# Expert jobs: the next expert's turned rows are split ahead of its weight tile in tiles 8, 10, 12 and 14

## The chip, the cores and the metric

The kernel runs on one core of one Trainium2 chip. The metric is the device time of one execution in microseconds (us); less is better. A time given for a kernel is the median of several executions, and the trace comes from one further execution taken with the profiler. Times in the trace count from the first instruction of that execution.

## The reference

The reference is a perceiver block on 16 sequences of 64 tokens of width 512 (1024 tokens in all). It has three residual stages, each on a layer norm of `x`:

```python
x = x + xattn(layernorm(x), ctx, ctx, ...)   # 16 heads of 64, 512 keys a sequence, layer norm of its own at the end
x = x + attn(layernorm(x), ...)              # 16 heads of 32, 3D rotary positions
x = x + ffn(layernorm(x), ...)               # 8 experts, the best 2 per token
```

The last one is the stage that this change touches:

```python
logits = xf @ Wr + br                        # xf: 1024 x 512, E = 8 experts
topv, _ = lax.top_k(logits, 2)
masked = jnp.where(logits >= topv[:, 1:2], logits, -jnp.inf)
weights = jax.nn.softmax(masked, axis=-1)
h = jax.nn.gelu(jnp.einsum('td,edh->eth', xf, W1) + b1[:, None, :], approximate=False)   # hidden width 2048
expert_out = jnp.einsum('eth,ehd->etd', h, W2) + b2[:, None, :]
out = jnp.einsum('etd,te->td', expert_out, weights)
```

## The kernel before

Every engine has a program of its own, written out in order (`tensor_program`, `vector_program`, `scalar_program`, `gpsimd_program`, `sync_program`), and the programs meet in semaphores. An engine works strictly through its list: what stands behind a waiting instruction waits too. Matrix products are made of float32 numbers split into a high and a low part in the type fp32r (three products: high by high, high by low, low by high). ScalarE writes the high part of an operand (a rounding copy), VectorE the low part (source minus high part). Each weight tile, each set of gathered rows and each hidden tile is split in this way.

The first 1180 us of the trace are the two attention stages and the routing, which writes for each expert a list of its tokens' rows to memory (`expert_rows`). Then come eight **jobs**, one for each expert `q`, numbered 0 to 7. A job is made for a number of rows (its width) that PE picks from `WIDTHS` by the count of this expert's tokens. In the profiled execution the matmuls of jobs 1, 3 and 5 are 224 wide, those of job 6 128, those of jobs 0, 2, 4 and 7 288, 512, 448 and 336.

A job goes over 16 **tiles** `i` of 128 hidden columns. In tile `i`:

- PE does `up(q, i)`: 12 matmuls (L448) of the expert's turned rows `xgT` with weight tile `Wh[i]` into a bank of PSUM, then `down(q, i-3)` (L809), 3 matmuls for each 128 rows of the width, of an older hidden tile, and in tiles 8, 10, 12 and 14 `turn_rows(q+1, c)`, c = 0 to 3: four transposes (L453) of 128 gathered rows `xg[c]` of the **next** expert, all into bank 7.
- ScalarE does the gelu of the bank (L1607), then in tiles 4 to 15 `split_next(q+1, i-4)`, the high part of the next expert's weight tile (L1314); in tiles 0 to 3 these are the last four of its own expert. In tiles 8, 10, 12 and 14 `rows_high(q+1, c)` (L1581) copies the turned rows out of bank 7.
- VectorE does the high and low part of the gelu's result (`hs`, L1275 and L1277), then `split_low` of the same weight tile (L888), and in tiles 8, 10, 12 and 14 `rows_low(q+1, c)` (L1254), the low part of the turned rows.

Which waits hold this together:

- `split_next` waits for the weight tile in its raw buffer (`raw`, four buffers in turn, loaded by SyncE's queue at L310) and for `down` to have left the slot `Wh[i]`. A raw buffer is loaded anew once `split_low` has read it.
- `rows_high` waits for the transposes of its chunk; `rows_low` waits for `rows_high`. Since all chunks are turned in bank 7, `turn_rows` of chunk c waits for `rows_low` of chunk c-1 (`xgT_lo`), and for its rows from memory.
- `up` of tile `i` waits for the gelu of tile `i-3`, `down(q, i-3)` for VectorE's L1277 of that hidden tile.

Of the kernel before, what the change touches and what calls it, by code (L numbers as in the profile page):

```python
# [19 lines left out]
def perceiver_block(nc, a, out):  # L20
# [17 lines left out]
    with ExitStack() as stack:  # L38
# [193 lines left out]
        def w_load(q, i):  # L232
            return L_E + q * NI + i
# [55 lines left out]
        def turned_at(i):  # L289
            return {8: 0, 10: 1, 12: 2, 14: 3}.get(i)  # L290
# [4 lines left out]
        def sent(t):  # L295

            return 16 * E * (t // 3 + 1) - (16 if t >= NT - 2 else 0)

        def turn_bank(q, c):

            return bank[3 + c] if q == 0 else bank[7]
# [580 lines left out]
        def vector_program(v):  # L882
            def split_lo(n, lo, hi):

                r = raw_of[n]
                src = raw[r][:] if len(lo.shape) == 2 else raw[r][:].rearrange("p (a b) -> p a b", a=lo.shape[1])
                v.wait_ge(split_hi, n + 1)
                v.tensor_tensor(lo, src, hi, ALU.subtract).then_inc(split_done[r], 1)  # L888
# [285 lines left out]
            def split_low(q, i):  # L1174
                split_lo(w_load(q, i), Wh[i][1][:], Wh[i][0][:])
# [74 lines left out]
            def rows_low(q, c):  # L1250
                src = turn_bank(q, c).rearrange("p (k z) -> p k z", k=KD)
                hi, lo = (x[:, :, c * P:(c + 1) * P] for x in xgT[q % 2])
                v.wait_ge(xgT_hi, CH * q + c + 1)
                v.tensor_tensor(lo, src, hi, ALU.subtract).then_inc(xgT_lo, 1)  # L1254

            def weighted(q):

                for c in range(CH):
                    if q == E - 1:  # L1260
                        v.wait_ge(y_ready, q + c + 1)
                    elif c == 0:
                        v.wait_ge(y_ready, q + 1 if q < E else q + CH)
                    else:
                        v.wait_ge(y_psum, NI * (q + 1))
                    v.wait_ge(ys_bias, CH * q + c + 1)
                    v.scalar_tensor_tensor(ys[c][:], bank[3 + c], weight(q, c), ys[c][:], ALU.mult, ALU.add).then_inc(y_done, 1)  # L1267

            def job(q, more):

                for i in range(NI):
                    n = NI * q + i
                    hi, lo = (x[:] for x in hs[n % HS])
                    v.wait_ge(gelu_done, n + 1)
                    v.tensor_copy(hi, gl[n % HS][:]).then_inc(h_hi, 1)  # L1275
                    v.wait_ge(h_hi, n + 1)
                    v.tensor_tensor(lo, gl[n % HS][:], hi, ALU.subtract).then_inc(h_lo, 1)  # L1277
                    if q == 0 and i < 3:
                        split_low(0, 10 + 2 * i)
                        split_low(0, 11 + 2 * i)  # L1280
                    if i > LAG and more:
                        split_low(q + 1, i - LAG - 1)
                    if i <= LAG and q % E:
                        split_low(q, NI + i - LAG - 1)
                    if more and turned_at(i) is not None:
                        rows_low(q + 1, turned_at(i))
                weighted(q)

            split_low(0, 3)
# [19 lines left out]
        def scalar_program(s):  # L1309
            def split_high(n, hi):  # L1310
                r = raw_of[n]
                src = raw[r][:] if len(hi.shape) == 2 else raw[r][:].rearrange("p (a b) -> p a b", a=hi.shape[1])
                s.wait_ge(raw_loaded[r], 16 * (raw_turn[n] + 1))
                s.activation(hi, src, ACT.Copy).then_inc(split_hi, 1)  # L1314
# [140 lines left out]
            def slot_left(i):  # L1455

                if i < 6:
                    s.wait_ge(qkv_psum, 3 * (NT - 1) + i // 2 + 1)
                elif i < 8:
                    s.wait_ge(nxT_psum, NT)  # L1460
                elif i == 8:
                    s.wait_ge(x1_bias, NT)
                    s.wait_ge(v2_done, NT)
                elif i == 9:
                    s.wait_ge(rope_done, 2 * NT)
                    s.wait_ge(s2_psum, 2 * NT)
                    s.wait_ge(o2_psum, NT)
                elif i == 10:
                    s.wait_ge(s2_psum, 2 * NT)
                    s.wait_ge(o2_psum, NT)  # L1470
                elif i < 13:
                    s.wait_ge(d_psum, NT)
                elif i == 13:
                    s.wait_ge(rows_sent[(NT - 1) % 3], sent(NT - 1))
                    s.wait_ge(rope_done, 2 * NT)
                    s.wait_ge(lg_psum, NT)
                elif i == 14:
                    s.wait_ge(rope_done, 2 * NT)
                    s.wait_ge(qkT_psum, 2 * NT)
                    s.wait_ge(lg_psum, NT)  # L1480
                else:
                    s.wait_ge(o2_psum, NT)
                    s.wait_ge(out_seeded, SEEDS)
                    s.wait_ge(e_norm, NT)

            def split_first(i):
                slot_left(i)
                split_high(w_load(0, i), Wh[i][0][:])
# [85 lines left out]
            def rows_high(q, c):  # L1574
                src = turn_bank(q, c).rearrange("p (k z) -> p k z", k=KD)
                if c == 0 and q >= 2:
                    s.wait_ge(h_psum, NI * (q - 1))
                elif c == 0:
                    s.wait_ge(qkv_psum, 3 * NT)
                s.wait_ge(xgT_psum, CH * q + c + 1)  # L1580
                s.activation(xgT[q % 2][0][:, :, c * P:(c + 1) * P], src, ACT.Copy).then_inc(xgT_hi, 1)  # L1581
# [16 lines left out]
            def job(q, more):  # L1598
                for i in range(NI):
                    n = NI * q + i  # L1600
                    col = (q % E) * NI + i
                    s.wait_ge(h_psum, n + 1)
                    if n == 0:
                        s.wait_ge(rows_sent[(NT - 2) % 3], sent(NT - 2))
                    if n >= HS:
                        s.wait_ge(y_psum, n - HS + 1)
                    s.activation(gl[n % HS][:], bank[n % 3], ACT.Gelu, bias=b1c[:, col:col + 1]).then_inc(gelu_done, 1)  # L1607
                    if q == 0 and i < 3:
                        split_first(10 + 2 * i)
                        split_first(11 + 2 * i)  # L1610
                    if i > LAG and more:
                        split_next(q + 1, i - LAG - 1)
                    if i <= LAG and q % E:
                        split_next(q, NI + i - LAG - 1)
                    if more and turned_at(i) is not None:
                        rows_high(q + 1, turned_at(i))
                weighted_bias(q, more)

            split_first(4)
# [286 lines left out]
```

## Time and profile before

| what | value |
|---|---|
| median of 3 executions | 1703.01 us |
| the three executions | 1698.38, 1703.01, 1706.31 us |
| the profiled execution's own time | 1704.67 us |
| its span, first to last instruction | 1702.7 us |
| mean granted TensorE clock | 0.974 |
| PE busy | 1618.6 us, 95% |
| VectorE (DVE) busy | 1184.5 us, 70% |
| ScalarE (ACT) busy | 970.7 us, 57% |
| GpSimd (POOL) busy | 355.7 us, 21% |

The span is the time between first and last instruction on the core; 2.0 us of the execution lie around it. In the rows further down, a row of a timeline has its start, its duration, the engine, the line, the operation, what it writes and reads, how many instructions it merges, and in brackets how long the engine was idle ahead of it and what it had waited for. The granted clock is the share of TensorE's full clock: 1.00 is 2.4 GHz, 0.50 is 1.2 GHz.

### The profile page before, as it was taken

How to read it: one execution, taken by the hardware profiler on the slowest of the kernel's cores; microseconds unless marked ns; L12 is line 12 of the kernel's file. 1: busy time of each engine (PE TensorE's matmuls, PEld its weight loads, DVE VectorE, ACT ScalarE, POOL GpSimd, SP SyncE). 2: the span in 40 equal slices, each digit the busy share in tenths (PEclk: the TensorE clock that was granted, in tenths of full speed). 3: DMA queues.
4: the chain of work that ended last, by engine and by line, in shares of the span. 5: the costliest groups of instructions: out<-in, count | busy, mean ns of one | idle time of the engine just before them, and what ended most of it. 6: DMA issues, size and time to landing. Idle time of an engine off the chain costs nothing. (4 is left out here: it accounts for less than half of the span.)

```text
span 1702.7 us, 27762 instructions
## 1 busy us (share of the span) xinstructions
PE 1618.6 (95%) x10730; PEld 1364.5 (80%) x10730; DVE 1184.5 (70%) x2032; ACT 970.7 (57%) x1792; POOL 355.7 (21%) x264
## 2 busy tenths in 40 slices
PE   7999999999999999999999979994899999999987
PEld 6888888888888888888888867773788888888876
DVE  4477777777778778777777776775778448548842
ACT  5566666766666666666666554442556346346631
POOL 4111111211212122112121134656211011011101
PEclk9999999999999999999999999995999999999799
DMA  6572111211211112113112152224757337537711
GB/s 228 191 132 55 50 38 51 94 63 38 82 63 46 61 63 81 38 51 105 51 38 81 38 171 64 65 78 149 245 156 215 131 89 243 159 86 246 217 39 21
DMA packets 60892, 175.20 MB, mean 103 GB/s; under 512 B 10996, under 2 KB 11380, under 8 KB 60192
## 3 DMA queue, kind: packets, MB, share of 16 engines
q1 hardware_dynamic: 45712, 143.97, 25.2%
q0 software_dynamic: 15024, 29.09, 7.9%
q8 instruction: 105, 1.72, 0.4%
q14 instruction: 51, 0.42, 0.1%
HBM read 155.63 MB, written 53.54 MB: 123 GB/s over the span
## 5 line engine op out<-in xcount | busy, mean ns | idle before, releaser
L448 PE MATMUL psum<-ctx,Wk 128*128 128x512 f32 x1536 | 384.6, 399 | 0.0
L448 PE MATMUL psum<-Wv,ctx 128*128 128x512 f32 x1536 | 368.9, 389 | 0.0
L448 PEld LDWEIGHTS psum<-Wv,ctx 128*128 128x128 f32 x1536 | 288.3, 188 | 59.9
L448 PEld LDWEIGHTS psum<-ctx,Wk 128*128 128x128 f32 x1536 | 279.1, 188 | 55.4
L1018 DVE SCALAR_TENSOR_TENSOR kT<-psum,bkc,kT 64x512 fp32r<-64x512 f32 x256 | 191.9, 749 | 151.5 <-ACT kT L1413 147.0
L448 PE MATMUL psum<-xgT,Wh 128*128 128x224 f32 (+5 forms) x1536 | 252.1, 318 | 14.1 <-issue 8.4
L448 PEld LDWEIGHTS psum<-xgT,Wh 128*128 128x128 f32 x1536 | 229.8, 198 | 33.6 <-issue 15.3
L809 PE MATMUL psum<-Wh,hs 128*128 128x512 f32 x981 | 246.6, 397 | 0.0
L1426 ACT ACTIVATE Pr<-Pr,smn 128x512 f32<-128x512 f32 x128 | 92.7, 724 | 241.4 <-DVE smn L1027 241.4
L1413 ACT ACTIVATE kT<-psum,bkc 64x512 fp32r<-64x512 f32 x256 | 174.3, 681 | 61.3 <-PE psum L448 57.9
L809 PEld LDWEIGHTS psum<-Wh,hs 128*128 128x128 f32 x981 | 181.5, 191 | 34.1 <-DVE hs L1277 0.3
L1607 ACT ACTIVATE gl<-psum,b1c 128x512 f32<-128x512 f32 x128 | 87.8, 687 | 202.0 <-PE psum L448 201.7
L1025 DVE TENSOR_TENSOR Pr<-psum,Pr 64x512 f32<-64x512 f32 x256 | 176.3, 689 | 8.0
L888 DVE TENSOR_TENSOR Wh<-raw,Wh 128x1024 fp32r<-128x1024 f32 x128 | 155.7, 1219 | 15.6 <-ACT Wh L1314 15.6
L1314 ACT ACTIVATE Wh<-raw 128x1024 fp32r<-128x1024 f32 x128 | 134.5, 1055 | 42.0 <-DMA raw<-in_W 41.8
L1643 POOL TENSOR_TENSOR Wo<-raw,Wo 128x1024 fp32r<-128x1024 f32 x32 | 76.8, 2400 | 386.3 <-ACT Wo L1314 386.3
L1421 ACT ACTIVATE Pr<-psum 64x512 f32<-64x512 f32 x256 | 151.9, 593 | 6.2
L1275 DVE CAST hs<-gl 128x512 fp32r<-128x512 f32 x128 | 55.3, 432 | 127.4 <-ACT gl L1607 126.9
L1643 POOL TENSOR_TENSOR ctx<-raw,ctx 128x1024 fp32r<-128x1024 f32 x32 | 76.8, 2400 | 288.5 <-ACT ctx L1314 288.5
L1797 POOL DMA_INDIRECT out_x<-xg,meta x22 | 36.3, 1649 | 382.3 <-DVE xg L1267 379.6
L955 DVE TENSOR_TENSOR V<-psum,bvb 128x512 f32<-128x512 f32 x128 | 88.5, 691 | 5.5 <-PE psum L448 1.5
L1277 DVE TENSOR_TENSOR hs<-gl,hs 128x512 fp32r<-128x512 f32 x128 | 88.7, 693 | 4.4
(155 smaller groups left out, 1975.9 us busy)
## 6 DMA issues: line engine op xcount, KB each, us to landing
raw<-in_W SPq DMA_DIRECT2D x128, 512.0 KB, 4.3
expert_rows<-in_spare_rows SPq DMA_DIRECT2D x16, 1042.0 KB, 5.7
raw<-in_ctxT SPq DMA_DIRECT2D x32, 512.0 KB, 3.7
raw<-in_Wo SPq DMA_DIRECT2D x32, 512.0 KB, 3.6
xg<-expert_rows POOLq DMA_DIRECT2D x32, 256.0 KB, 6.2
out_x<-x SPq DMA_DIRECT2D x12, 256.0 KB, 2.4
xs<-in_x SPq DMA_DIRECT2D x4, 512.0 KB, 6.0
raw<-in_Wq SPq DMA_DIRECT2D x4, 512.0 KB, 6.6
```

The costliest lines, as they stand in the source:

```text
L448: mm = pe.matmul(dst, l, r, start=n == 0, stop=n == len(pairs) - 1)
L809: mm = pe.matmul(bank[3 + c], hr[x][:, c * P:(c + 1) * P], Wh[i][y][:, 512:1024], start=i == 0 and m == 0, stop=i == NI - 1 and m == 2)
L888: v.tensor_tensor(lo, src, hi, ALU.subtract).then_inc(split_done[r], 1)
L955: v.tensor_tensor(V[u % 2][:, kt, :], bank[2 + n % 2], bvb[:, cs], ALU.add).then_inc(v_done, 1)
L1018: v.scalar_tensor_tensor(k[other, :], bank[n % 2][own, :], bkc[own, j:j + 1], k[own, :], ALU.add, ALU.subtract).then_inc(k_lo, 1)
L1025: v.tensor_tensor(Pr[m % 2][rows, :], bank[4 + h][rows, :], Pr[m % 2][rows, :], ALU.add).then_inc(s_max, 1)
L1277: v.tensor_tensor(lo, gl[n % HS][:], hi, ALU.subtract).then_inc(h_lo, 1)
L1314: s.activation(hi, src, ACT.Copy).then_inc(split_hi, 1)
L1413: s.activation(kT[n % 2][h][own, :], bank[n % 2][own, :], ACT.Identity, bias=bkc[own, j:j + 1]).then_inc(k_hi, 1)
L1421: s.activation(Pr[m % 2][rows, :], bank[4 + h][other, :], ACT.Copy).then_inc(s_exp, 1)
L1426: s.activation(Pr[m % 2][:], Pr[m % 2][:], ACT.Exp, bias=smn[:, r:r + 1], accum_out=ssum[:, r:r + 1]).then_inc(s_exp, 1)
L1643: g.tensor_tensor(lo, src, hi, ALU.subtract).then_inc(split_done[r], 1)
```

## The change

In tiles 8, 10, 12 and 14 of a job, which have both a weight tile to split and a chunk of turned rows, the two change places on ScalarE and on VectorE: the turned rows come first, the weight tile second. Nothing is added or removed, and PE's, GpSimd's and SyncE's programs are the same.

```diff
@@ VectorE, job(q, more), loop over i
+                    if more and turned_at(i) is not None:
+                        rows_low(q + 1, turned_at(i))
                     if i > LAG and more:
                         split_low(q + 1, i - LAG - 1)
                     if i <= LAG and q % E:
                         split_low(q, NI + i - LAG - 1)
-                    if more and turned_at(i) is not None:
-                        rows_low(q + 1, turned_at(i))
@@ ScalarE, job(q, more), loop over i
+                    if more and turned_at(i) is not None:
+                        rows_high(q + 1, turned_at(i))
                     if i > LAG and more:
                         split_next(q + 1, i - LAG - 1)
                     if i <= LAG and q % E:
                         split_next(q, NI + i - LAG - 1)
-                    if more and turned_at(i) is not None:
-                        rows_high(q + 1, turned_at(i))
```

ScalarE, tiles 7 to 10 of job 6, as the program of before has them. `gl` is a gelu's result, `Wh40` the high part of the next expert's weight tile 4, `raw` its raw buffer, `xgT10` the high part of the next expert's turned rows.

```order
L1607 ACTIVATE gl3_203<-psum,b1c_50 128x512
L1314 ACTIVATE Wh30_174<-raw1_84 128x1024
L1607 ACTIVATE gl0_200<-psum,b1c_50 128x512
L1314 ACTIVATE Wh40_176<-raw2_85 128x1024
L1581 ACTIVATE xgT10_162<-psum 128x4x128
L1607 ACTIVATE gl1_201<-psum,b1c_50 128x512
L1314 ACTIVATE Wh50_178<-raw3_86 128x1024
L1607 ACTIVATE gl2_202<-psum,b1c_50 128x512
L1314 ACTIVATE Wh60_180<-raw0_83 128x1024
L1581 ACTIVATE xgT10_162<-psum 128x4x128
```

The same place on ScalarE in the changed program:

```order
L1607 ACTIVATE gl3_203<-psum,b1c_50 128x512
L1314 ACTIVATE Wh30_174<-raw1_84 128x1024
L1607 ACTIVATE gl0_200<-psum,b1c_50 128x512
L1581 ACTIVATE xgT10_162<-psum 128x4x128
L1314 ACTIVATE Wh40_176<-raw2_85 128x1024
L1607 ACTIVATE gl1_201<-psum,b1c_50 128x512
L1314 ACTIVATE Wh50_178<-raw3_86 128x1024
L1607 ACTIVATE gl2_202<-psum,b1c_50 128x512
L1581 ACTIVATE xgT10_162<-psum 128x4x128
L1314 ACTIVATE Wh60_180<-raw0_83 128x1024
```

The copy of the turned rows (L1581) moved ahead of weight tiles 4 and 6 and directly behind the gelu; weight tiles 3 and 5 stay.

VectorE, tiles 8 and 9 of job 6, before. `hs` are the two parts of the hidden tile, `Wh41` and `xgT11` low parts.

```order
L888 TENSOR_TENSOR Wh31_175<-raw1_84,Wh30_174 128x1024
L1275 CAST hs00_204<-gl0_200 128x512
L1277 TENSOR_TENSOR hs01_205<-gl0_200,hs00_204 128x512
L888 TENSOR_TENSOR Wh41_177<-raw2_85,Wh40_176 128x1024
L1254 TENSOR_TENSOR xgT11_163<-psum,xgT10_162 128x4x128
L1275 CAST hs10_206<-gl1_201 128x512
```

The same place on VectorE in the changed program:

```order
L888 TENSOR_TENSOR Wh31_175<-raw1_84,Wh30_174 128x1024
L1275 CAST hs00_204<-gl0_200 128x512
L1277 TENSOR_TENSOR hs01_205<-gl0_200,hs00_204 128x512
L1254 TENSOR_TENSOR xgT11_163<-psum,xgT10_162 128x4x128
L888 TENSOR_TENSOR Wh41_177<-raw2_85,Wh40_176 128x1024
L1275 CAST hs10_206<-gl1_201 128x512
```

The low part of the turned rows (L1254), for which PE's next four transposes wait, moved ahead of the low part of the weight tile (L888), for which the raw buffer's next load waits.

## Rows read from the trace of the kernel before

**Rows 1.** The page, part 1: engine, busy us, share of the span, instructions.
```profile
PE 1618.6 (95%) x10730; PEld 1364.5 (80%) x10730; DVE 1184.5 (70%) x2032; ACT 970.7 (57%) x1792; POOL 355.7 (21%) x264
```

**Rows 2.** Waits, 1226 to 1572 us (jobs 0 to 5): total us, times, longest.
```profile
ACT xgT L1581 <- PE psum L453: 18.1, 20, 1.6
ACT Wh L1314 <- DMA raw<-in_W: 16.4, 11, 3.2
...
PE psum L453 <- DMA xg<-expert_rows: 0.3, 1, 0.3
```

**Rows 3.** Waits, 1566 to 1625 us (job 6), same columns.
```profile
PE psum L453 <- DVE xgT L1254: 4.0, 1, 4.0
```

**Rows 4.** Chain of waits, 1560 to 1640 us: start, us, what.
```profile
1587.35 8.33 DMA raw<-in_W
```

**Rows 5.** Timeline of ScalarE, job 6, tiles 7 to 8.
```profile
1593.11 1.06 ACT L1314 ACTIVATE Wh<-raw 128x1024 fp32r<-128x1024 f32 x1 [4.33 <-DMA raw<-in_W]
1594.07 0.67 ACT L1607 ACTIVATE gl<-psum,b1c 128x512 f32<-128x512 f32 x1
1595.76 1.06 ACT L1314 ACTIVATE Wh<-raw 128x1024 fp32r<-128x1024 f32 x1 [1.01 <-DMA raw<-in_W]
1596.72 0.58 ACT L1581 ACTIVATE xgT<-psum 128x512 fp32r<-128x512 f32 x1
```

**Rows 6.** Timeline of VectorE, job 6, tile 8 and the start of tile 9.
```profile
1595.34 0.42 DVE L1275 CAST hs<-gl 128x512 fp32r<-128x512 f32 x1
1595.80 0.69 DVE L1277 TENSOR_TENSOR hs<-gl,hs 128x512 fp32r<-128x512 f32 x1
1596.85 1.23 DVE L888 TENSOR_TENSOR Wh<-raw,Wh 128x1024 fp32r<-128x1024 f32 x1 [0.36 <-ACT Wh L1314]
1597.99 0.68 DVE L1254 TENSOR_TENSOR xgT<-psum,xgT 128x512 fp32r<-128x512 f32 x1
1598.59 0.42 DVE L1275 CAST hs<-gl 128x512 fp32r<-128x512 f32 x1
```

**Rows 7.** Timeline of PE, job 6: turn of chunk 0, the last down, turn of chunk 1.
```profile
1590.17 0.60 PE L453 MATMUL psum<-ident,xg 128*128 128x128 f32 x4
...
1593.93 0.92 PE L809 MATMUL psum<-Wh,hs 128*128 128x512 f32 x3
1598.82 1.08 PE L453 MATMUL psum<-ident,xg 128*128 128x128 f32 x4 [3.97 <-DVE xgT L1254]
```

**Rows 8.** Stretches of job 6; behind the busy times: granted clock, DMA share, GB/s.
```profile
1594.00:1597.00 3.00, 0.85 (x4) 0.36 (x3) 2.41 (x4) 1.99 (x4) 0.00 (x0) 1.00 0.87 341
1597.00:1598.80 1.80, 0.00 (x0) 0.01 (x1) 1.80 (x3) 1.80 (x4) 0.00 (x0) 0.54 0.71 282
1598.80:1617.00 18.20, 18.18 (x74) 16.83 (x75) 13.55 (x20) 9.17 (x13) 0.00 (x0) 0.50 0.55 175
1617.00:1621.00 4.00, 4.00 (x23) 3.38 (x23) 2.94 (x5) 2.92 (x5) 0.00 (x0) 0.92 0.37 134
```

**Rows 9.** Timeline of PE, job 0: two other idle gaps.
```profile
1200.27 2.43 PE L448 MATMUL psum<-xgT,Wh 128*128 128x288 f32 x12 [3.13 <-ACT gl L1607]
...
1215.97 1.82 PE L448 MATMUL psum<-xgT,Wh 128*128 128x288 f32 x12 [1.80 <-ACT gl L1607]
```

**Rows 10.** Stretches of job 0 around and behind these gaps, columns as in Rows 8.
```profile
1200.00:1205.00 5.00, 4.73 (x19) 4.25 (x20) 1.79 (x3) 1.43 (x3) 0.26 (x1) 0.66 0.91 323
1210.00:1216.00 6.00, 4.20 (x25) 3.41 (x23) 3.29 (x5) 2.87 (x4) 0.00 (x0) 1.00 1.00 320
1216.00:1221.00 5.00, 5.00 (x31) 4.56 (x32) 4.90 (x9) 4.51 (x6) 0.00 (x0) 1.00 0.85 317
```

**Rows 11.** Timeline of VectorE, job 6, tiles 1 and 2: start of each tile.
```profile
1578.32 0.42 DVE L1275 CAST hs<-gl 128x512 fp32r<-128x512 f32 x1
...
1580.52 0.42 DVE L1275 CAST hs<-gl 128x512 fp32r<-128x512 f32 x1
```

**Rows 12.** Timeline of PE: first product of job 7.
```profile
1627.58 9.38 PE L448 MATMUL psum<-xgT,Wh 128*128 128x336 f32 x48 [6.00 <-issue]
```

**Rows 13.** Timeline of ScalarE, job 1, tile 10 and the gelu of tile 11.
```profile
1287.11 1.06 ACT L1314 ACTIVATE Wh<-raw 128x1024 fp32r<-128x1024 f32 x1
1288.13 0.60 ACT L1581 ACTIVATE xgT<-psum 128x512 fp32r<-128x512 f32 x1
1289.46 0.69 ACT L1607 ACTIVATE gl<-psum,b1c 128x512 f32<-128x512 f32 x1 [0.73 <-PE psum L448]
```

## The prediction

> **What bounds the kernel now.** I read the share of each engine first: PE is busy 95% of the span and no other engine is above 70% [rows 1]. So a change of order on ScalarE and VectorE can only pay where PE waits for them, and can only cost where it makes PE wait. Next I read the waits of the stretch that the change touches, the jobs. In jobs 0 to 5, from tile 8 of job 0 on, the list holds many waits of ScalarE and VectorE for PE, and on PE's own side next to nothing: 0.3 us for gathered rows [rows 2]. In job 6 there is one that matters: PE waits 4.0 us, once, for L1254, the low part of the turned rows [rows 3]. Job 7 turns no rows for a next expert, so the edit is not in it.
>
> The timelines of the three engines tell how that wait comes about. Job 6 is the narrowest, so it asks for weight tiles fastest, and for a while the loads do not keep up: in the chain of waits a load stands for 8.33 us [rows 4]. ScalarE stands 4.33 us ahead of weight tile 3, then does gelu 8, then stands another 1.01 us ahead of weight tile 4; only behind that comes the copy of the turned rows at 1596.72 [rows 5]. Yet chunk 0 had been turned since 1590.17 + 0.60 = 1590.77 [rows 7]. VectorE repeats the order: hidden tile 8, weight tile 4, then the rows at 1597.99 to 1598.67 [rows 6]. PE ended its last down at 1594.85, could go no further than the transposes of chunk 1, and started them at 1598.82, 0.15 after VectorE's end [rows 7]. The last thing to come is thus one weight tile on ScalarE, one weight tile on VectorE, and behind them the two instructions that PE needs. This is the pair that the change turns round.
>
> The stall has a second price. Until 1597 the granted clock is 1.00 (2.4 GHz); in 1597.0 to 1598.8 it is 0.54, so it fell to 1.2 GHz at about 1597.1, some 2.3 us after PE fell idle, and it is 0.50 for the whole 18.2 us behind, in which PE is busy for 18.18 [rows 8]. In the last 4 us of the job it is 0.92. The working below rests on these stretches.
>
> **The change in job 6, step by step.** What stands ahead of tile 8 is the same, so gelu 8 still starts at 1594.07 and hidden tile 8 at 1595.34.
> - ScalarE: the copy of the rows waits for nothing, since chunk 0 is turned. It starts when gelu 8 lets it, about 1594.65, and ends at about 1595.25. Weight tile 4 starts when its load lands, 1595.76, as before: the copy lies wholly in the 1.01 us of idle time [rows 5]. Its cost is nothing here. Without that cover it would push gelu 9 by its own 0.6 us, and PE is not waiting for that gelu.
> - VectorE: L1277 starts at 1595.80, and its successor starts about 0.60 behind it, as 1597.99 to 1598.59 shows for one of the same kind [rows 6]. L1254 therefore runs from 1596.40 to 1597.08 instead of 1597.99 to 1598.67. It fills the 0.36 us that VectorE stood idle there, and L888 comes at 1597.00 instead of 1596.85. The raw buffer is free 0.15 us later, and the next hidden tile starts at 1597.00 + 1.14 = 1598.14 instead of 1598.59.
> - PE: the transposes of chunk 1 start at 1597.08 + 0.15 = 1597.23, which is 1.59 us earlier. The stall goes from 3.97 to 2.38 us. It does not vanish, since what is late next is hidden tile 8 on VectorE (1595.34 to 1596.49), which stands ahead of the rows and itself comes from the 4.33 us wait for weight tile 3, in a tile that the change leaves as it is.
>
> **What the clock does with 1.59 us.** In this profile the clock fell at 1597.1 and PE would come back at 1597.23, so by this execution it falls all the same. The two nearest gaps bound the question: after one of 3.13 us the stretch has 0.66, so there too the clock fell; after one of 1.80 us it stayed at 1.00 [rows 9, 10]. At 2.38 us either can be. I take the fall as the likelier, because 2.38 us still reaches past the point, 2.3 us into the idle time, at which it fell here. With the fall, all that follows until the clock is back is PE at half speed, so 1.59 us less of waiting is 1.59 us less of time if the clock comes back at the same place in the work. If it comes back at the same time, 1.59 us of work at half clock has been taken from a rest that is done at full clock, where it is worth 0.8. I take the middle, **1.2 us**, and keep 0.8 and 1.6 as bounds.
>
> The Trainium skill (TensorE: Matmul & The Clock Gate, Part 1: The HAM clock gate) has it that the low clock is the state of rest, and that sustained matmul activity lifts it. By that rule PE, busy from 1598.8 on, would soon be at full clock again, and a fall would cost no more than a few us; the row of 18.2 us at 0.50 with PE busy throughout says otherwise for this narrow job, and the measurement decides. By the page, the rival without a fall would be worth little more than the 1.6 us of waiting.
>
> **The change in the other jobs.** Take tile 10 of job 1. Before, weight tile 6 ran at 1287.11 to 1288.17 while PE was still turning, the copy followed at 1288.13 to 1288.73, and gelu 11 came at 1289.46 after 0.73 us of idle time [rows 13]. Now ScalarE stands until 1288.13, then does the copy, then the weight tile to about 1289.7, and gelu 11 starts some 0.15 late. PE needs that gelu for `up` of tile 14, three tiles on, so this costs nothing. On VectorE the hidden tile that follows starts up to 0.6 us later, and `down` asks for it three tiles later too. The weight tiles of the next expert are wanted a job later, and a raw buffer freed up to 1.2 us later is wanted again only four tiles on. In the 20 places of this kind where ScalarE waited for the turn, 18.1 us in all and at most 1.6 [rows 2], the weight tile used to be cover for a wait and now isn't; since ScalarE is busy 57% and VectorE 70% [rows 1], I put all of it at **0**, with at most 0.3 us a job either way if a job's end catches one.
>
> **The sum.** The profiled execution took 1704.67 us (span 1702.7 and 2.0 around it). 1704.67 - 1.2 = 1703.5. It lies 1.66 us above the median of 1703.01, so the forecast for a median is 1703.01 - 1.2 = **1701.8 us**.
>
> **The rivals.**
> 1. *The clock does not fall.* Then job 6 goes on at full clock and its pace is VectorE's, not PE's. One tile on VectorE is 1580.52 - 1578.32 = 2.20 us [rows 11], a tile with turned rows 0.60 more. From the cast of tile 9 at 1598.14 to that of tile 15 are six tiles, three of them with rows: 13.2 + 1.8 = 15.0, so 1613.1. Its low part ends 1.15 later at 1614.3, and the last down takes PE to about 1615.2. Before, PE ended the job at 1627.58 - 6.00 = 1621.58 [rows 12]. That is 6.4 us less, 1703.01 - 6.4 = 1696.6 us. For it: 2.38 us is nearer to the gap of 1.80 that left the clock alone than to 3.97. Against it: the point of the fall above.
> 2. *No change.* The stall of 4 us hangs on when single loads land (1593.1 and 1595.8). In an execution where weight tile 4 has landed by the time of gelu 8, the order costs only two weight splits less cover; where a row chunk lands later still, PE waits for that in both kernels. Then nothing moves: 1703.0.
> 3. *Slower: the clock falls and comes back too late.* Before, it came back just in time for the last 4.0 us of job 6. Those 4.0 us less the 0.8 that has been done earlier are 3.2 at full clock and 6.4 at half: job 6 would end at 1617.6 + 6.4 = 1624.0, which is 2.4 us later than before, and the time is 1705.4. It decides at one point: whether the mix of narrow products, downs and transposes, shifted by 1.6 us, brings the clock back before the job ends. For it: the clock stayed low for 18 us of busy PE, so its return is a near thing. Against it: the shift brings more work ahead of the same point.
>
> **How the numbers follow.** The forecast of 1701.8 has a chance of 0.50, rival 1 (1696.6) 0.25, rival 2 (1703.0) 0.13, rival 3 (1705.4) 0.12. The three executions of before spread from 1698.4 to 1706.3, so a median of a few moves by some 2 us by itself. The range takes in rival 1 and rival 3 with a little of that on each side: 1695.5 to 1706.0. A measurement of this kernel can tell about 0.5%, 8.5 us, from no change. A gain over 8.5 us needs rival 1 and a lucky 2 us more: 0.07. A loss over 8.5 us needs rival 3 and several us more: 0.03. The rest, 0.90, is within 0.5%.
>
> **What would show it.** In the profile of the changed kernel, the copy L1581 of job 6, tile 8, should start directly behind its gelu, inside the idle time ahead of the weight tile. PE's wait for L1254 should be about 2.4 us instead of 4.0. Then the granted clock decides: 0.50 over most of the rest of job 6 is the forecast; 1.00, with hidden tiles 2.2 to 2.8 us apart and the job done some 6 us sooner, is rival 1; a job 6 that ends at 0.50 is rival 3. In jobs 0 to 5 PE should show no new idle time. Wrong would be a wait of PE for a gelu or a hidden tile behind tiles 8, 10, 12 or 14 in these jobs, or loads that land so differently that job 6 stalls at another place.

## The result and the profile after

The changed kernel took 1711.61 us (median of 20 executions, 1703.56 to 1722.00) where the kernel before took 1702.99 beside it. The ratio is 1.0050 with a 95% interval of 1.0035 to 1.0065: it is slower, by 0.5%. The forecast was 1701.8 in a range of 1695.5 to 1706.0, so both the size and the side were wrong. One of the 20 executions of the kernel before took 2305.67 us and one of the 12 of e7 below 2036.34 us, far outside the rest, and the ratios leave such executions out.

The profiled execution of the changed kernel took 1720.48 us, span 1718.6. It lies in the upper part of its own 20, so its 15.8 us above the profiled execution of before show where the time goes, not how much of it goes in the median.

The page's first part tells that PE, the engine that bounds the kernel, had 9 us more to do although it has the same instructions [rows 1], which means that more of them ran at the low clock:

```profile
PE 1627.6 (95%) x10730; PEld 1373.1 (80%) x10730; DVE 1187.7 (69%) x2032; ACT 968.8 (56%) x1792; POOL 355.7 (21%) x264
```

The waits that the prediction dealt with are not where the rest is. The list of waits of the changed kernel, 1226 to 1660 us, has no wait of PE for L1254, but this (what waited for what, total us, times, longest):

```profile
PE psum L448 <- issue: 15.8, 5, 6.3
```

"Issue" is idle time in which the engine waited for nothing that the profile shows. The timeline of PE shows where these are: ahead of the first product of jobs 1, 2, 4, 6 and 7. First the kernel before (job 7 is in [rows 12]):

```profile
1261.17 5.59 PE L448 MATMUL psum<-xgT,Wh 128*128 128x224 f32 x48 [0.48 <-issue]
...
1307.47 11.17 PE L448 MATMUL psum<-xgT,Wh 128*128 128x512 f32 x48 [0.85 <-issue]
...
1442.84 9.96 PE L448 MATMUL psum<-xgT,Wh 128*128 128x448 f32 x48 [0.77 <-issue]
...
1573.83 5.54 PE L448 MATMUL psum<-xgT,Wh 128*128 128x128 f32 x48 [0.27 <-issue]
```

and then the changed one:

```profile
1261.23 5.59 PE L448 MATMUL psum<-xgT,Wh 128*128 128x224 f32 x48 [1.70 <-issue]
...
1309.47 13.97 PE L448 MATMUL psum<-xgT,Wh 128*128 128x512 f32 x48 [2.79 <-issue]
...
1449.59 9.96 PE L448 MATMUL psum<-xgT,Wh 128*128 128x448 f32 x48 [2.38 <-issue]
...
1583.50 8.97 PE L448 MATMUL psum<-xgT,Wh 128*128 128x128 f32 x48 [2.60 <-issue]
...
1643.65 8.93 PE L448 MATMUL psum<-xgT,Wh 128*128 128x336 f32 x48 [6.29 <-issue]
```

The first four of these gaps have grown from 2.37 to 9.47 us. In two of the rows the duration has grown too: 48 products of 512 columns take 13.97 us instead of 11.17, 48 of 128 take 8.97 instead of 5.54. The clock fell in or behind the gap (in job 6 it was still 1.00 when the gap ended, and 0.50 from 1585 on). In stretches of the changed kernel (PE busy first, granted clock third from the end) job 6 looks so:

```profile
1580.90:1583.50 2.60, 0.00 (x1) 0.03 (x1) 2.11 (x4) 0.00 (x0) 1.65 (x1) 1.00 0.42 158
...
1585.00:1622.00 37.00, 37.00 (x152) 34.48 (x151) 24.34 (x33) 17.61 (x22) 3.95 (x7) 0.50 0.60 188
1623.00:1633.00 10.00, 10.00 (x78) 9.39 (x77) 9.49 (x14) 8.36 (x12) 0.00 (x0) 1.00 0.48 156
```

```profile
L863 PEldq COMPARE_BRANCH  x1: 3291/3291/3291, 1304.0 to 1304.0; - x1
...
L858 PEldq COMPARE_BRANCH  x1: 3591/3591/3591, 1570.1 to 1570.1; - x1
```

```profile
L863 PEldq COMPARE_BRANCH  x1: 4571/4571/4571, 1304.7 to 1304.7; - x1
...
L858 PEldq COMPARE_BRANCH  x1: 5271/5271/5271, 1578.1 to 1578.1; - x1
```

So in the kernel before these two branches take 3.3 and 3.6 us (the others at the ends of jobs 0 to 5 3.35 to 4.39). In the DMA records one packet of 16 KB of PE's instructions lies within each of them. PE's matmuls of the last tiles, which are queued ahead of the branch, hide most of it. The Trainium skill (Advanced Engine Details and Errata, Control Flow Timing) gives a compare-and-branch about 108 ns; the trace has 65 ns for most of those that are not taken and thirty to fifty times the page's figure for the one that goes to the next job's block. The measurement decides.

Two things have changed at the end of job 1, and both come out of tile 14. The timeline of VectorE at the end of job 1, before and then changed:

```profile
1299.84 1.22 DVE L888 TENSOR_TENSOR Wh<-raw,Wh 128x1024 fp32r<-128x1024 f32 x1
1300.97 0.68 DVE L1254 TENSOR_TENSOR xgT<-psum,xgT 128x512 fp32r<-128x512 f32 x1
1301.93 0.43 DVE L1275 CAST hs<-gl 128x512 fp32r<-128x512 f32 x1 [0.28 <-ACT gl L1607]
1302.39 0.69 DVE L1277 TENSOR_TENSOR hs<-gl,hs 128x512 fp32r<-128x512 f32 x1
```

```profile
1300.57 0.69 DVE L1254 TENSOR_TENSOR xgT<-psum,xgT 128x512 fp32r<-128x512 f32 x1 [0.44 <-ACT xgT L1581]
1301.52 1.23 DVE L888 TENSOR_TENSOR Wh<-raw,Wh 128x1024 fp32r<-128x1024 f32 x1 [0.26 <-ACT Wh L1314]
1302.66 0.42 DVE L1275 CAST hs<-gl 128x512 fp32r<-128x512 f32 x1
1303.11 0.69 DVE L1277 TENSOR_TENSOR hs<-gl,hs 128x512 fp32r<-128x512 f32 x1
```

and ScalarE there, changed:

```profile
1299.94 0.60 ACT L1581 ACTIVATE xgT<-psum 128x512 fp32r<-128x512 f32 x1 [1.15 <-PE psum L453]
1300.43 1.05 ACT L1314 ACTIVATE Wh<-raw 128x1024 fp32r<-128x1024 f32 x1
1301.38 0.68 ACT L1607 ACTIVATE gl<-psum,b1c 128x512 f32<-128x512 f32 x1
```

ScalarE now stands 1.15 us for the turn before it may touch weight tile 10, so both engines finish that tile about 1.7 us later. VectorE starts hidden tile 15 at 1302.66 instead of 1301.93 and is done with it 0.72 us later. PE's program passes its last wait, the one for that tile, only then, and reaches the branch 1.95 us ahead of the end of its matmuls instead of 2.61; the branch starts 0.94 us behind VectorE's end in both kernels. That is the first part. The second: the raw buffer is free later, and the load of weight tile 14 is issued at 1302.77 instead of 1301.08. Timelines of SyncE's queue, 1300 to 1306 us, before and changed:

```profile
1301.08 3.50 SPq L310 DMA_DIRECT2D raw<-in_W  x2
```

```profile
1302.77 2.53 SPq L310 DMA_DIRECT2D raw<-in_W  x2
```

In the DMA records the packet of instructions started 0.92 us into the branch and took 0.88 us before; in the changed kernel it started at 1.12 and took 1.94. At the end of job 5 it started 1.24 us into the branch and took 0.93 before, 2.10 and 1.75 in the changed kernel. So a fetch with a load close ahead of it starts later, or takes longer, or both. What follows the packet is 1.2 to 1.5 us in every such branch of every kernel here.

The gap is what the branch takes less how long ahead it is reached, plus 0.16 us. So the 7.1 us by which the four gaps have grown can be split. The branches of jobs 1, 3 and 5 are reached 0.66, 0.66 and 0.65 us later, 2.0 us in all; those of jobs 0, 1, 3 and 5 take 1.22, 1.28, 0.96 and 1.68 us longer, 5.1 us in all. The branch of job 0 is reached 4.08 us ahead in every kernel of this document, so the late hidden tile plays no part there. The branches at the ends of the wide jobs 2 and 4 took 3.4 to 3.8 us, were reached 3.4 to 3.9 us ahead, and left no gap in either kernel.

### The profile page after: what moved, and what is told of

It reads as the page before. It is cut to its first block and busy times, and to the rows that moved or that the text cites. A ratio compares the mean times of both kernels' runs of the same rounds, so it can differ in the third digit from the quotient of the medians.

```text
span 1718.6 us, 27762 instructions
## 1 busy us (share of the span) xinstructions
PE 1627.6 (95%) x10730; PEld 1373.1 (80%) x10730; DVE 1187.7 (69%) x2032; ACT 968.8 (56%) x1792; POOL 355.7 (21%) x264
## 5 line engine op out<-in xcount | busy, mean ns | idle before, releaser
L448 PE MATMUL psum<-xgT,Wh 128*128 128x224 f32 (+5 forms) x1536 | 261.2, 326 | 22.0 <-issue 15.8
L448 PEld LDWEIGHTS psum<-xgT,Wh 128*128 128x128 f32 x1536 | 238.9, 205 | 42.3 <-issue 22.9
L888 DVE TENSOR_TENSOR Wh<-raw,Wh 128x1024 fp32r<-128x1024 f32 x128 | 155.8, 1220 | 18.7 <-ACT Wh L1314 18.7
L1277 DVE TENSOR_TENSOR hs<-gl,hs 128x512 fp32r<-128x512 f32 x128 | 88.6, 692 | 4.4
```

Of the source, the lines that this page charges most:

```text
L448: mm = pe.matmul(dst, l, r, start=n == 0, stop=n == len(pairs) - 1)
```

## The experiments

The theory has these two parts and a third: (1) hidden tile 15 is late, so the branch is reached late; (2) later loads lie on the fetch, so the branch takes longer; (3) the longer gap lets the clock fall, and in the narrow job 6 it then stays low for long. The rivals of this theory: the loss is spread over all four tiles (raw buffers freed later everywhere), or it is the clock's alone and tied to no place.

For all kernels, from their profiles: PE's idle gap in us at the ends of jobs 0, 1, 3 and 5, how long before the end of PE's matmuls the branch of job 1 began and how long it took, the length of job 6 from its first gelu to that of job 7, and the ratio of the times to the kernel before on the same chip. Gaps, branches and job 6 are those of one profiled execution for each kernel; only the ratio rests on many.

| kernel | gaps, ends of jobs 0, 1, 3, 5 | branch of job 1: ahead, took | job 6 | ratio (95%) |
|---|---|---|---|---|
| before | 0.48, 0.85, 0.77, 0.27 | 2.61, 3.29 | 55.9 | 1 |
| changed | 1.70, 2.79, 2.38, 2.60 | 1.95, 4.57 | 62.0 | 1.0050 (1.0035 to 1.0065) |
| e12, changed again | 1.30, 3.03, 2.00, 1.56 | 1.95, 4.81 | 53.4 | 1.0046 (1.0024 to 1.0068) |
| e1, swap in 8, 10, 12 | 0.43, 1.04, 1.16, 0.74 | 2.61, 3.49 | 48.5 | 0.9999 (0.9982 to 1.0015) |
| e2, swap in 14 | 0.78, 2.92, 1.88, 1.56 | 1.94, 4.65 | 51.1 | 1.0065 (1.0041 to 1.0089) |
| e7, swap on VectorE only | 0.80, 1.90, 2.07, 1.25 | 2.20, 3.94 | 49.8 | 1.0038 (1.0014 to 1.0063) |
| e3, changed, loads held at 1, 3 | 1.19, 1.57, 1.42, 2.67 | 1.85, 3.26 | 62.0 | 1.0050 (1.0028 to 1.0073) |
| e6, changed, loads held at 1, 3, 5 | 0.88, 1.89, 1.58, 0.70 | 1.95, 3.67 | 49.3 | 1.0011 (0.9991 to 1.0031) |
| e4, before, loads held at 1, 3 | 0.50, 1.09, 0.76, 0.33 | 2.52, 3.44 | 49.0 | 1.0000 (0.9982 to 1.0018) |
| e5, e4 and hidden tile 15 late | 0.60, 1.69, 1.83, 0.34 | 1.92, 3.44 | 49.6 | 1.0012 (0.9995 to 1.0029) |
| e8, swap, tile 10 behind 15 | 0.62, 1.21, 1.08, 0.30 | 2.61, 3.65 | 49.7 | 0.9976 (0.9959 to 0.9992) |
| e11, tile 10 behind 15 alone | 0.58, 0.91, 1.31, 0.20 | 2.52, 3.26 | 50.4 | 0.9994 (0.9974 to 1.0014) |
| e9, e1 and no drain | 0.44, 1.55, 1.35, 0.96 | 2.52, 3.90 | 48.6 | 1.0005 (0.9983 to 1.0026) |
| e10, e8 and no drain | 0.74, 1.17, 0.86, 0.06 | 2.61, 3.61 | 47.7 | 0.9966 (0.9951 to 0.9982) |

### Which tile: e1 and e2

Each keeps one part of the swap; the diff is against the kernel before, on both engines, and `(8, 10, 12)` is `(14,)` in the second:

```diff
+                    if more and turned_at(i) is not None and i in (8, 10, 12):
+                        rows_low(q + 1, turned_at(i))
                     if i > LAG and more:
                         split_low(q + 1, i - LAG - 1)
...
-                    if more and turned_at(i) is not None:
+                    if more and turned_at(i) is not None and i not in (8, 10, 12):
                         rows_low(q + 1, turned_at(i))
```

> The swap stays in tiles 8, 10 and 12 and is undone in tile 14. Theory A (the job's end): the loss comes from tile 14 alone, where the later hidden tile 15 lets PE reach its branch to the next job later and the later loads lie on the fetch of that job's instructions. Then PE's gaps at the ends of jobs 0, 1, 3 and 5 are again 0.5, 0.85, 0.8 and 0.3 us (they are 1.7, 2.8, 2.4 and 2.6 in the changed kernel), the branches take 3.3 to 4.4 us, and the time is that of the kernel before or 1 to 3 us less. Rival B (all four tiles count, through raw buffers freed later): three quarters of the loss of 8.6 us stay, about 1709 us.

> The swap stands in tile 14 only. Theory A: all of the loss, 1709 to 1714 us, with gaps of 1.7 to 2.8 us at the ends of jobs 0, 1, 3 and 5. Rival B: a quarter of it, about 1705 us, with gaps that are not much longer than before. Rival C (the loss is the clock's, by chance of where it falls, and not tied to one place): no pattern of gaps.

The swap of three tiles costs nothing that can be measured (0.9999) and that of tile 14 alone costs all of it (1.0065). The gaps follow: 1.04 us at the end of job 1 in e1, 2.92 in e2. (At the end of job 5 e1 has 0.74 where 0.3 was expected; its branch there took 4.04 us.) The rival of four equal tiles is out, and so is the one of the clock alone, since e2's gaps stand at the same places as the changed kernel's. The gain that the first half of theory A allowed for e1, 1 to 3 us, is not to be seen.

### The loads on the fetch: e3, e4 and e6

In e3 (the changed kernel) and e4 (the kernel before) SyncE holds two loads back until PE has done the first product of the next job; e6 is e3 with the end of job 5 as well, `q in (2, 4, 6)`:

```diff
                 for i in range(NI):
+                    if q in (2, 4) and i == 14:
+                        sp.wait_ge(h_psum, NI * q + 1)
                     fetch(w_load(q, i), w12[q, i])
```

> The changed kernel, but the loads of the next expert's weight tiles 14 and 15 at the ends of jobs 1 and 3 wait until PE has done the first product of the next job; jobs 0 and 5 are left as they are. Theory A has two parts: the branch is reached 0.65 us later, and it takes 1.0 to 1.7 us longer because loads share the DMA engines with the fetch of instructions. If the second part holds, the branches at the ends of jobs 1 and 3 take 3.3 us (4.6 and 4.3 in the changed kernel) and the gaps there are about 1.5 us, while the branch at the end of job 5 stays at 4.5 to 5.3 us. If loads don't matter, all stay as long as in the changed kernel.

> The kernel before with the same hold at the ends of jobs 1 and 3. Theory A: branches of 3.3 us as before or a little less, gaps of 0.6 to 0.9 us, time within 0.2% of the kernel before. If the hold itself costs something (a weight tile that comes too late for ScalarE in tile 2 of jobs 2 and 4) it shows here as a wait of ScalarE for a load.

The branch at the end of job 1, e3, then the one at the end of job 5, which was left as it was:

```profile
L865 PEldq COMPARE_BRANCH  x1: 3258/3258/3258, 1306.1 to 1306.1; - x1
...
L860 PEldq COMPARE_BRANCH  x1: 5335/5335/5335, 1574.6 to 1574.6; - x1
```

Where the loads are held the branch takes what it takes in the kernel before, 3.26 us, and 3.33 at the end of job 3 (4.57 and 4.31 in the changed kernel); where they are not, 5.34. One execution holds both cases. The gap at the end of job 1 is 1.57 us, and what is left of it against 0.85 is the first part, the late branch (1.85 us ahead instead of 2.61). The time did not improve, 1.0050: the gap of 2.67 us at the end of job 5 was still there, and job 6 took 62.0 us as in the changed kernel. e4 shows that holding by itself costs nothing that can be measured.

> The changed kernel with the loads held at the end of job 5 as well. Theory: the branch there takes 3.6 us instead of 5.3, the gap is about 1.5 us instead of 2.6, the clock does not fall ahead of job 6, and job 6 takes 48 to 51 us instead of 62. The median comes to 1704 to 1709 us: most of the loss goes with the clock, and what stays is 0.6 us at each of jobs 0, 1, 3 and 5 and the collision at job 0. If the clock falls all the same, job 6 stays at 62 us in the profile and the median at 1711 or more.

The branch of job 5 and PE's first product of job 6 in e6:

```profile
L860 PEldq COMPARE_BRANCH  x1: 3347/3347/3347, 1576.5 to 1576.5; - x1
```

```profile
1580.02 5.55 PE L450 MATMUL psum<-xgT,Wh 128*128 128x128 f32 x48 [0.70 <-issue]
```

and the first part of job 6, stretches of e6:

```profile
1582.00:1594.00 12.00, 12.00 (x94) 11.40 (x94) 10.96 (x15) 8.65 (x12) 4.34 (x6) 1.00 0.94 290
1594.00:1610.00 16.00, 13.73 (x102) 11.97 (x101) 15.35 (x23) 12.30 (x18) 0.94 (x2) 1.00 0.84 295
```

The branch is at 3.35 us, the gap at 0.70 (less than the 1.5 expected, since this branch is reached 2.82 us ahead, those of jobs 1 and 3 1.95 and 2.09), the clock stays at 1.00 and job 6 takes 49.3 us. The ratio went from 1.0050 to 1.0011, which is no longer told from 1; the two intervals barely overlap. Of the two kernels only two loads at the end of job 5 differ in when they may start, so the pair shows part (2), and part (3) in the two profiles. Loads are not all of it: with the loads held, the branches of e5 and e6 at the ends of jobs 1 and 3 still took 3.44 to 3.79 us.

How much of the loss goes through the clock can be read from the single executions, each of which has its mean granted clock on record. In the changed kernel 9 of 20 executions have 0.970 or less, and in e12, the same kernel, 2 of 12; these took 1714.7 to 1722.0 us. The four of the 20 with 0.977 or more took 1703.6 to 1706.3 us, within the spread of the kernel before. Of the 103 executions of the kernel before beside the experiments, 2 have 0.970 or less; of e3's 10 six, of e6's 12 one. So most of what the median lost comes with a lower clock. At which gap it fell in each execution is not on record, except in the profiled ones.

### The late hidden tile: e5 and e7

e5 adds to e4 one VectorE instruction that nobody needs:

```diff
                     v.wait_ge(gelu_done, n + 1)
+                    if i == 15 and q in (1, 3):
+                        v.bn_stats(bst[:, q // 2, :], gl[n % HS][:])
                     v.tensor_copy(hi, gl[n % HS][:]).then_inc(h_hi, 1)
```

> The kernel before with the loads held at the ends of jobs 1 and 3 (so that no load lies on the fetch) and with one needless VectorE instruction of some 0.6 us (statistics of gelu 15, whose result nobody reads) ahead of the cast of hidden tile 15 in jobs 1 and 3. Theory: PE's program reaches its branch only when the low part of hidden tile 15 is there, and PE's queue has nothing behind it, so the gap at the end of the job grows by the delay, one to one: from 1.09 and 0.76 us with the loads held to about 1.7 and 1.4 us, with branches still of 3.3 to 3.5 us; job 5 stays at 0.3. If there is slack between hidden tile 15 and the branch, the gaps stay at 1.1 and 0.8 us.

The gap at the end of job 1 is 1.69 us against 1.09 in e4, with the same branch of 3.44 us, which is reached 0.60 us closer to the end of the matmuls (1.92 for 2.52). So there is no slack between hidden tile 15 and the next job: a delay there is paid one to one. In job 3 the branch was reached 0.60 us closer too (2.13 for 2.73) and took 3.79 for 3.33 on top, for a gap of 1.83 against 0.76; job 5, without the instruction, has 0.34.

e7 has the swap on VectorE and ScalarE's order of before:

> The swap on VectorE alone, ScalarE in the order of the kernel before. Theory: hidden tile 15 is late in the changed kernel because weight tile 10 comes late on ScalarE (it stands there for the turn first) and VectorE's low part of it is queued ahead of hidden tile 15. With ScalarE's old order the cast of hidden tile 15 at the end of job 1 comes some 0.3 us later than before instead of 0.6 to 0.7, PE reaches the branch about 2.3 us ahead of its last matmul, and the loss is about half: median 0 to 0.3% above the kernel before. If VectorE's order alone makes it, the 1.95 us and the full loss stay.

The branch is reached 2.20 us ahead, between the 2.61 of before and the 1.95 of the change, so 0.41 of the 0.66 us is VectorE's order and 0.25 ScalarE's, which stands for the turn with the weight tile behind it; at the end of job 3 it is 0.31 and 0.35. About half each. The ratio of 1.0038 is above the 1.003 I allowed; the branches of jobs 1 and 3 took 3.94 and 4.34 us, so the loads lie on the fetch here too.

### A better order: e8, e11, e9 and e10

e8 keeps all four swaps and takes weight tile 10 out of the way of hidden tile 15, on both engines:

```diff
-                    if i > LAG and more:
+                    if i == 15 and more:
+                        split_low(q + 1, 10)
+                    if i > LAG and i != 14 and more:
                         split_low(q + 1, i - LAG - 1)
```

> The change with one difference: in tile 14 ScalarE and VectorE split the turned rows only, and weight tile 10 follows in tile 15, behind hidden tile 15. So hidden tile 15 is as early as in the kernel before, and the loads of weight tiles 14 and 15 are later than in any kernel so far. Theory: PE reaches its branch 2.6 us ahead of its last matmul at the end of job 1, as in the kernel before, not 1.95 as in the changed one; what is left of the loss is the collision of loads and fetch, branches of 4 to 5 us and gaps of 1.5 to 2.2 us. Median 1703 to 1711 us. If only the late hidden tile counts, gaps are 0.3 to 0.9 us and the median is 1703 to 1706.

> The kernel before, no swap, with weight tile 10 split in tile 15 behind hidden tile 15 on both engines. It tells whether the gain of the version with both (0.24%) is the swap's or this edit's. Theory: before the change, hidden tile 15 waited for its gelu and not for VectorE, so this edit alone gains nothing: 1.000, and PE's stall for the turned rows of job 6 stays at 2 to 4 us. If it gains as much as the two together, the swap has no part in the gain.

e8 is faster than the kernel before, 0.9976 (0.9959 to 0.9992). The branch is reached 2.61 us ahead as before, and the collision that I expected to remain is small: a branch of 3.65 us, and gaps of 1.21, 1.08 and 0.30. That was a miss on my side. The branch at the end of job 1 and the loads behind it, e8 (branches by line, then SyncE's queue, 1307.7 to 1312 us):

```profile
L863 PEldq COMPARE_BRANCH  x1: 3651/3651/3651, 1307.6 to 1307.6; - x1
```

```profile
1307.83 1.46 SPq L310 DMA_DIRECT2D raw<-in_W  x2
```

What counts is where the load before the branch lies. In e8 the two loads are issued 0.23 and 1.36 us behind the start of the branch, and the packet of instructions starts 0.91 us into it, as in the kernel before. In the kernel before the last load ahead of the branch is issued 2.94, 2.82 and 2.07 us ahead of it at the ends of jobs 1, 3 and 5, and the branches take 3.29, 3.35 and 3.59 us; in the changed kernel 1.97, 1.85 and 1.10 us ahead, and they take 4.57, 4.31 and 5.27. So a load half a microsecond to two ahead of the branch is more in the way than an earlier or a later one. It is no sharp border: e9, with loads 2.79 and 2.71 us ahead at the ends of jobs 1 and 3, has branches of 3.90 and 3.91. e11, without the swap, gives 0.9994 (0.9974 to 1.0014), and its stall for the turned rows of job 6 is 2.4 us against 1.9 in e8. The two intervals overlap, so it is not shown that the swap has a share in e8's gain.

e9 and e10 replace PE's wait for its own last product at the end of a job of at most 128 rows, and are e1 and e8 otherwise:

```diff
                 if i == NI - 1 and width <= P:
-                    pe.wait_ge(y_psum, n + 1)
-                    pe.sem_inc(y_ready, 1)
+                    pe.matmul(bank[(n + 1) % 3][:, 0:P], hr[0][:, 0:P], Wh[i][0][:, 512:512 + P],
+                              start=True, stop=True).then_inc(y_ready, 1)
```

> The swap in tiles 8, 10 and 12 only, and at the end of a job of at most 128 rows PE no longer waits for its own last product before it raises the signal for VectorE; a small spare matmul behind it raises the signal, so PE's program reaches the branch some 1.7 us earlier. Theory: the gap at the end of job 6 goes from 5.6 to 6.0 us to some 4.0 us. Time 1 to 2 us below the swap of three tiles alone, about 1702 us against 1705 for the kernel before. If the branch is held up by something else, the gap stays at 5.6.

> All together: the swap in four tiles, weight tile 10 behind hidden tile 15, and the spare matmul in place of PE's wait at the end of a narrow job. The first two gave 0.24% (4 us), the third took the gap at the end of job 6 from about 6.0 to 3.6 us. Expected: 1699 to 1702 us where the kernel before has 1706, ratio 0.996 to 0.998. If the clock takes it back, no better than the version without the spare matmul.

The gap at the end of job 6 went from 6.00 us [rows 12] to 3.59 in e9, and to 3.06 in two pieces in e10 (PE's timeline):

```profile
1621.64 3.93 PE L448 MATMUL psum<-xgT,Wh 128*128 128x336 f32 x14 [1.93 <-issue]
1626.69 3.54 PE L448 MATMUL psum<-xgT,Wh 128*128 128x336 f32 x22 [1.13 <-issue]
```

e9 was no faster (1.0005, interval 0.9983 to 1.0026), so alone this edit is not told from nothing; three of its 12 executions had a mean granted clock of 0.968 to 0.970 and took 1714 to 1716 us. e10 is the fastest of all: 1697.58 us against 1703.32 for the kernel before beside it, 0.9966 (0.9951 to 0.9982). It beats both kernels.

### The change once more: e12

> The changed kernel again, beside the three others on one chip. If the loss is its own and not one chip's, the median is 0.3 to 0.7% above the kernel before, with gaps of 1.2 to 2.8 us at the ends of jobs 1, 3 and 5.

It gave 1.0046, so the loss is the kernel's and not one chip's. In this profile the clock did not fall ahead of job 6 (gap 1.56 us), but it did at the ends of jobs 1 and 3, for 3.4 us each time. PE's wait for L1254 in job 6, in e12 and, for comparison, in e2, whose tile 8 has the order of before (both from 1570 to 1640 us):

```profile
PE psum L453 <- DVE xgT L1254: 1.7, 1, 1.7
```

```profile
PE psum L453 <- DVE xgT L1254: 3.0, 1, 3.0
```

## Why the prediction was wrong

**What bounds the kernel, and the stall in job 6: right, with the size off.** The stall of PE for the turned rows is real, and the swap shortens it. PE's waits for L1254 in job 6, in all, are 4.0 (before), 3.0 (e2), 2.6 (e4), 2.7 (e5) and 2.4 us (e11) with the old order in tile 8. With the swap on both engines, where the job ran at full clock up to there, they are 1.9 (e1), 1.7 (e12), 2.2 (e6), 1.9 (e8), 2.8 (e9) and 1.9 (e10). That is about 0.9 us by the means, 2.9 to 2.1, where I had 1.59. In e1 and e6 another 2.8 us of PE's time went into waits for hidden tiles (L1277) instead. In the changed kernel's own profile there was no wait for L1254 at all, since PE was at half clock.

The profile that I started from was also not typical. In e4, e5 and e11, whose tiles 8 to 12 of job 6 are in the order of before, the job took 49.0, 49.6 and 50.4 us, not 55.9, and the low clock in it lasted 7 to 10 us, not 20. So the execution that I worked from had more to win than these three. The kernel with just the three swaps, e1, gave 0.9999: what was right is too small to be measured.

**The step that failed** is the one on the other jobs: "On VectorE the hidden tile that follows starts up to 0.6 us later, and `down` asks for it three tiles later too", with the sum "I put all of it at 0". The delay was sized nearly rightly for the cast (0.73 us at the end of job 1) and the cover was wrongly named. For tiles 8, 10 and 12 the cover is three tiles, and e1 shows that it suffices. For tile 14 the tile that follows is the last, the downs of tiles 12 to 15 stand in a row in PE's queue, and behind them is not a matmul but a branch of 3.3 us that PE's sequencer can only reach when hidden tile 15 is there. In the kernel before this path was already on the critical path, by 0.27 to 0.85 us a job. The list of waits for jobs 0 to 5 had the line; I read over it, saying that on PE's side there was "next to nothing", because its releaser was called "issue":

```profile
PE psum L448 <- issue: 2.1, 3, 0.8
```

The other half of that step cost more. "A raw buffer freed up to 1.2 us later is wanted again only four tiles on" (it was 1.7 us at the end of job 1) was right for ScalarE, which did not wait more for loads (23.4 us before, 10.9 in the changed kernel, both from 1226 to 1660 us). It left out who else uses the DMA engines at the time to which a load is moved: the fetch of PE's instructions. Where I had 0, the profile of the changed kernel has 7.1 us of longer gaps, 2.0 from branches reached later and 5.1 from branches that took longer, and the low clock behind them.

**The clock.** I counted the clock's fall only at the stall in tile 8. It fell at the new gaps instead. By the profile of the changed kernel, the four gaps hold 7.1 us more than before, and the jobs behind them the rest of what is lost from job 0 to job 7, some 10 us, of which job 6 alone took 6.1. What rival 3 took for granted, that after a fall in the narrow job the low clock lasts long, came true (37 us at 0.50), but at another place and from another cause. The sign of being wrong named in the prediction, "loads that land so differently that job 6 stalls at another place", comes near to it, and is not it.

**The rivals.** None had the mechanism. The one on the slower side was placed in job 6, tile 8, at 1705.4 and with 0.12, and the chance of over 0.5% slower was 0.03. A rival built from the question "what does PE do next after tile 15" would have had its price from [rows 12], where the same gap is 6.0 us long because there the branch is reached after the last product.

## What to carry to other kernels

At the end of a loop body with code of its own for each pass, ask when the sequencer reaches the branch, not only when the engine's operands are there: what the last waits hang on may have no cover left, and an operation that is harmless in the middle of the loop can cost its full delay there (0.60 us for 0.60 in e5). Where the list of waits says "issue" ahead of the first product of a block, look for a branch of the sequencer there, and for loads that are issued just ahead of it; moving such a load by a microsecond or two, either way, took one to two microseconds off the branch here. When a reorder is to serve one place, make it at that place only, and test the last pass by itself.

## What the runs showed of the hardware

- A taken branch of PE's sequencer to the next job's block took 3.26 to 3.79 us at the ends of jobs 1, 3 and 5 where the loads were held back (e3 to e6). It took 3.93 to 5.27 us there in the two profiles of the changed kernel, with a load issued 1.1 to 2.0 us ahead of it, and 5.61 and 5.21 at the end of job 0, with one 0.62 us ahead. In e8, whose loads are issued 0.2 to 1.1 us behind its start, it took 3.63 to 3.65. Most branches that are not taken have 65 ns. Queued matmuls run on meanwhile.
- One packet of 16 KB of PE's instructions lies in each of these branches; from its end to the end of the branch it was 1.2 to 1.5 us, with and without loads. What the loads change is when the packet starts (0.9 to 3.4 us into the branch) and how long it takes (0.88 to 1.94).
- The granted clock fell to 1.2 GHz at gaps of 2.60 us and more at the ends of jobs (2.60, 2.67, 2.79, 2.92, 3.03), and once at 2.00 (e12, end of job 3) and once at 1.90 (e7, end of job 1), in some cases only after PE was at work again, up to 1.6 us after it. It did not fall at others of 1.56 to 2.38 (2.38 in the changed kernel, 1.88 in e2, 1.83 in e5). In this range the length of a gap alone does not settle it.
- Once low at the start of the 128 row job, it stayed low for 37 us in two kernels (changed and e3), while ahead of the wide jobs 2 and 4 it came back after 3.4 to 6.8 us (48 products in 13.97 us instead of 11.17). The Trainium skill (TensorE: Matmul & The Clock Gate, Part 1: The HAM clock gate) says that sustained activity lifts the low clock. The rows of the wide jobs agree with that; the row of 37.00 us busy at 0.50 does not, and the measurement decides. Why it stayed low there was not tested.
